# Attention scores and their row maxima from float32r parts of q and k: even and odd heads on the two row halves of the TensorE array, issued in pairs

## What is computed

```python
x = x + _L0_conv_ref(_gn(x), L0_conv_w_qkv, L0_conv_w_o)
x = x + _L1_conv_ref(_gn(x), L1_conv_w1, L1_conv_b1, L1_conv_w2, L1_conv_b2, L1_conv_bias_w, L1_conv_bias_b)

def _L0_conv_ref(x, w_qkv, w_o):
    ...
    attn = jnp.einsum('bhqd,bhkd->bhqk', q, k) * scale      # scale = 16 ** -0.5, n = 1024 tokens
    attn = jax.nn.softmax(attn, axis=-1)
    out = jnp.einsum('bhqk,bhkd->bhqd', attn, v)
    out = out.swapaxes(1, 2).reshape(bs, n, c)
    return out @ w_o
```

## Time and profile before

| | |
|---|---|
| median of three runs | 1689.3 us (1689.0 to 1699.71) |
| profiled execution, first to last instruction (the only time of it that is given) | 1693.3 us |
| TensorE (PE) busy | 1619.6 us, 96% |
| DVE busy | 1242.5 us, 73% |
| ACT busy | 980.5 us, 58% |
| POOL busy | 235.2 us, 14% |
| first score matmul | 71.4 us |
| start of the last score matmul | 1596.2 us |

### The profile page before, as it was taken

How to read it: one execution, slowest core, us unless ns; L and a number is a source line. 1 busy time by engine, 2 the same in 40 slices (tenths; PEclk the granted TensorE clock), 3 DMA queues, 4 the chain that set the end, 5 groups by cost and what they waited for, 6 DMA issues and landing times.

```text
span 1693.3 us, 28191 instructions
## 1 busy us (share of the span) xinstructions
PE 1619.6 (96%) x8580; PEld 692.3 (41%) x8580; DVE 1242.5 (73%) x2236; ACT 980.5 (58%) x1837; POOL 235.2 (14%) x297
## 2 busy tenths in 40 slices
PE   8999999999999999999999999999999999999877
PEld 4233334344343444344343443434444444434345
DVE  2887888777778767877678777877788777787132
ACT  4275776665656655666556665666566666666401
POOL 3001001410104001130013100141011300030010
PEclk9699999999999999999999999999999999999989
DMA  4501113134313134041240430422430412310323
GB/s 109 82 20 38 16 39 82 27 58 83 81 22 58 35 78 101 3 73 48 49 101 2 83 73 14 101 32 54 83 78 7 74 47 48 82 27 22 66 42 77
DMA packets 110733, 93.81 MB, mean 55 GB/s; under 512 B 27632, under 2 KB 96624, under 8 KB 110576
## 3 DMA queue, kind: packets, MB, share of 16 engines
q1 hardware_dynamic: 110576, 91.86, 27.2%
HBM read 14.32 MB, written 6.29 MB: 12 GB/s over the span
## 4 chain that ended last, share of the span: by engine, by line
PE 67%; issue 14%; DVE 6%; POOL 4%; SPq 3%; DMA 3%; ACT 1%; POOLq 0%; DVEq 0%; ACTq 0%
PE o_acc L1168 17%; PE scores L1134 16%; PE max_tiles L1148 15%; DVE row_max L902 3%; PE prep_bank L1239 3%; PE prep_bank L1191 2%; PE post_bank L1303 2%; PE post_bank L1297 2%; SPq L584 2%; PE post_bank L1203 2%; PE post_bank L1310 2%; DMA rows_b<-rows_a 1%; PE post_bank L1289 1%; PE post_bank L1210 1%; PE post_bank L1191 1%
## 5 line engine op out<-in xcount | busy, mean ns | idle before, releaser
L902 DVE TENSOR_REDUCE row_max<-max_tiles 128x1 f32<-128x512 f32 x1536 | 972.6, 680 | 208.7 <-PE max_tiles L1148 205.5
L805 ACT ACTIVATE probs<-scores 128x512 f32<-128x512 f32 x1536 | 837.2, 596 | 368.6 <-PE scores L1134 362.9
L1134 PE MATMUL scores<-q_stack,k_stack 98*128 98x512 bf16 x1536 | 587.3, 384 | 3.1 <-ACT probs L805 2.6
L1148 PE MATMUL max_tiles<-k_stack,q_stack 96*128 96x512 bf16 x1536 | 581.8, 388 | 6.0 <-DVE row_max L902 4.3
L1168 PE MATMUL o_acc<-probs,v_aug 128*32 128x512 f32 x3072 | 413.1, 610 | 13.1 <-ACT o_raw L813 11.9
L1134 PEld LDWEIGHTS scores<-q_stack,k_stack 98*128 98x128 bf16 x1536 | 150.3, 98 | 381.7 <-ACT probs L805 254.7
L1148 PEld LDWEIGHTS max_tiles<-k_stack,q_stack 96*128 96x128 bf16 x1536 | 152.7, 99 | 181.3 <-DVE row_max L902 76.0
L463 POOL TENSOR_TENSOR o_raw<-o_raw,inv_all 128x1024 f32<-128x1024 f32 x23 | 54.2, 2356 | 763.8 <-DVE inv_all L930 763.8
L1168 PEld LDWEIGHTS o_acc<-probs,v_aug 128*32 128x32 f32 x3072 | 60.8, 108 | 160.0 <-issue 144.2
L735 POOL TENSOR_TENSOR qk_parts<-rest,qk_parts 128x512 bf16<-128x512 f32 x48 | 55.5, 1156 | 404.3 <-DVE qk_parts L960 404.3
L1239 PE MATMUL prep_bank<-xt,w_qk 96*128 96x512 f32 x172 | 80.8, 592 | 0.0
(11 more groups left out here) (220 smaller groups left out, 1114.4 us busy)
## 6 DMA issues: line engine op xcount, KB each, us to landing
q_stack<-qk_parts SPq DMA_DIRECT2D x288, 64.0 KB, 2.6
k_stack<-qk_parts SPq DMA_DIRECT2D x144, 128.0 KB, 4.5
rows_b<-rows_a SPq DMA_DIRECT2D x128, 96.0 KB, 3.2
spec_b<-spec_a SPq DMA_DIRECT2D x64, 102.0 KB, 2.3
x_in<-in_x_dram SPq DMA_DIRECT2D x8, 768.0 KB, 5.8
o_t<-o_raw SPq DMA_DIRECT2D x96, 64.0 KB, 2.4
x<-in_x_dram SPq DMA_DIRECT2D x8, 768.0 KB, 6.8
rows_b<-spec_b SPq DMA_DIRECT2D x32, 192.0 KB, 3.3
```

The costliest lines, as they stand in the source:

```text
L805: nc.scalar.activation(probs[:, GH * (s % 2) + h, :], scores[:, n % SCORE_BANKS, :], ACT.Exp, scale=SCALE).then_inc(probs_made, 1)
L902: nc.vector.tensor_reduce(row_max[:, which, pair_of_half:pair_of_half + 1], max_tiles[:, no % MAX_BANKS, :], AX.X, ALU.max).then_inc(max_t ...
L1134: mm(scores[:, n % SCORE_BANKS, :], k_stack[:, head, P * kt:P * (kt + 1)], q_stack[:, g, half, h, :], start=True, stop=True).then_inc(scor ...
L1148: mm(max_tiles[:, no % MAX_BANKS, :], q_stack[0:KQ, g, half, h, P * qt:P * (qt + 1)], k_stack[0:KQ, GH * g + h, HALF * which:HALF * (which ...
```

## The change

- q and k are cut into two float32r parts in place of three bf16 parts. Three products of parts are stacked (`KQ` = 48), with the two shift rows 50.
- A stack holds two heads: even heads on partitions 0 to 49, odd heads on 64 to 113. Each score or maximum matmul then uses 64 rows of the array, the lower or the upper half.
- The order on PE becomes score, score, maximum, maximum, product with v, middle jobs, score, score, maximum, maximum. The two maximum matmuls of a pair are the odd and the even head for the same queries and keys (`max_unit`).
- The evacuation of a q/k job has two operations: ACT writes part 0, DVE writes part 1 straight from the bank. `rest`, the cast and the POOL operation are gone. `stack` waits for DVE in place of POOL.
- `shifts` takes four transfers in place of two. `stack` still takes six, of the same number of bytes.
- The rows of ones come from one DVE memset of `k_stack` in the prologue in place of 12 ACT instructions.

```diff
-Q_PARTS = (0, 0, 0, 1, 1, 2)
-K_PARTS = (0, 1, 2, 0, 1, 0)
+Q_PARTS = (0, 0, 1)
+K_PARTS = (0, 1, 0)
 KQ = HD * len(Q_PARTS)
...
-        qk_parts = sb("qk_parts", [P, 3, 3, TOK], BF16)
-        rest = sb("rest", [P, 2, HALF])
-        q_stack = sb("q_stack", [KQ + 2, NG, 2, GH, HALF], BF16)
-        k_stack = sb("k_stack", [KQ + 2, NH, TOK], BF16)
+        qk_parts = sb("qk_parts", [P, 2, 3, TOK], F32R)
+        q_stack = sb("q_stack", [P, NG, 2, GH // 2, HALF], F32R)
+        k_stack = sb("k_stack", [P, NH // 2, TOK], F32R)
...
+        def max_unit(unit, i):
+
+            half, m = divmod(unit, HUNITS)
+            hp, qt = divmod(m, NT // 2)
+            return half, hp, qt, 1 - i % 2, i // 2
...
-                for n in range(2):
-                    sp.dma_start(q_stack[KQ + n:KQ + n + 1, g, half, :, :],
-                                 shift[:, n, :]).then_inc(shift_in, 16)
+                for n, odd in itertools.product(range(2), range(2)):
+                    row = 64 * odd + KQ + n
+                    sp.dma_start(q_stack[row:row + 1, g, half, :, :].bitcast(F32),
+                                 shift[HMAX // 2 * odd:HMAX // 2 * (odd + 1), n, :].bitcast(F32)
+                                 ).then_inc(shift_in, 16)
...
-            def last_part(b, k):
-
-                pool.wait_ge(part1_done, 6 * b + k + 1)
-                cols = slice(HALF * (k % 2), HALF * (k % 2 + 1))
-                nc.gpsimd.tensor_tensor(qk_parts[:, 2, k // 2, cols], rest[:, k % 2, :],
-                                        qk_parts[:, 1, k // 2, cols], ALU.subtract
-                                        ).then_inc(part2_done, 1)
...
-                head = GH * g + h
-                mm(scores[:, n % SCORE_BANKS, :], k_stack[:, head, P * kt:P * (kt + 1)],
-                   q_stack[:, g, half, h, :],
+                hp, odd = divmod(h, 2)
+                rows = slice(64 * odd, 64 * odd + KQ + 2)
+                mm(scores[:, n % SCORE_BANKS, :], k_stack[rows, 2 * g + hp, P * kt:P * (kt + 1)],
+                   q_stack[rows, g, half, hp, :],
                    start=True, stop=True).then_inc(scores_made, 1)
...
-                    for tile in tiles[0:1]:
+                    score_tile(b, g, s, 0)
+                    score_tile(b, g, s, 1)
+                    for tile in tiles[0:2]:
                         max_tile(*tile)
-                    score_tile(b, g, s, 0)
-                    for tile in tiles[1:2]:
-                        max_tile(*tile)
-                    score_tile(b, g, s, 1)
...
                     score_tile(b, g, s, 2)
-                    for tile in tiles[2:3]:
-                        max_tile(*tile)
                     score_tile(b, g, s, 3)
-                    for tile in tiles[3:]:
+                    for tile in tiles[2:]:
                         max_tile(*tile)
```

More of the change, by code:

```diff
@@ L856, in prologue @@
             def prologue():
-                act.wait_ge(cleared, 3)
-                for head in range(NH):
-                    nc.scalar.activation(k_stack[KQ:KQ + 2, head, :], inv_all[KQ:KQ + 2, :],
-                                         ACT.Identity, bias=1.0).then_inc(stack_ones, 1)
                 for no, (kind, k) in enumerate(PREP):
```

144 lines of the change are left out of this document (65 added, 79 removed).

## The result

The changed kernel takes **1747.2 us**, the median of four runs (1737.6 to 1761.0), against 1690.8 us for the kernel before on the same chip (1689.0 to 1699.7): a ratio of **1.033, 95% interval 1.027 to 1.038**. It is slower, where 1649 us was forecast. The profiled execution has a span of 1759.1 us, 65.8 more than the one of before.

The account below looks back on a forecast made before the run. PE was taken to bound the kernel, with the score loop close behind. Batches together -39 us and prologue -1.6 took the profiled 1693.3 to 1653; less a 4.0 offset, 1649 us, range 1600 to 1735 (likeliest case 1620 to 1672).

Parts of the forecast that it names:

- The score loop: Round of score matmuls and exponentials through two score banks: 2.88 us, rising to about 3.15 in a step without jobs.
- open loads: Weight loads on PE not hidden behind a running matmul: 0.04 us per step, between 0 and 0.15.
- The free room for a first job: PE's wait for exponentials, from third score to the next step's second: 0.95 us of a first job costs nothing.
- its turns: PE's changes between tile shapes: its own step becomes about 2.1 us with them, 1.96 without.
- The sum of a full batch: 48 steps of 3.15 us plus middle jobs, first-job excess and additions: 193.3 us, 10 less than 203.4.
- the 5.8 us added for ACT's copies and for DVE: Added to a full batch: 2.8 us for ACT evacuating middle jobs between exponentials, 3 us for DVE's bunched work.
- the 10 for DVE in batch 0: Added to batch 0 for DVE, making it 173 us, 7.4 more than before.
- the 10 us of batch 3: Gain computed for full batch 3 and given to each of the four batches in the loop.
- The clock: PE's granted clock should stay full, as in batch 7 at 1.00 despite waits; a fall would make the forecast wrong.
- Batch 7: The batch whose last 11 steps have no maximum matmuls: its time stays within 1 us.
- The prologue: Cast and POOL operation ahead of the first stack go: 0.42 + 1.16 = 1.6 us won.
- everything meets everything: Rival: PE, ACT and DVE nearly level, maximum matmuls' bank waits hold up the product with v; 3.3 us, 1718; chance 0.12.

Follow-up runs that it names:

- e5: Changed kernel with the first maximum pair moved between score 0 and score 1, ahead of the second score matmul: 1731.1 us, ratio 1.021 to the kernel before.
- e1: Kernel before, bf16 on all rows, with only PE's order changed to score, score, maximum, maximum: 1750.8 us, ratio 1.035.
- e9: Changed kernel with every score and maximum matmul on all 128 rows, none side by side: 1788.4 us, ratio 1.058 to the kernel before.
- e12: Kernel before, bf16 and its own order, with score and maximum matmuls on only 34 and 32 rows: 2948.3 us, ratio 1.74.
- e3: Changed kernel with all score and maximum matmuls on the lower half of the array, none side by side: 2372.5 us, ratio 1.40 to the kernel before.

## Why the prediction was wrong

**The score loop: right mechanism, mis-sized.** The prediction took 2.88 us + 0.22 for the maximum pair + 0.04 for open loads = 3.15. Measured: 3.33. The pair costs 0.24 (e5 against the changed kernel, and 3.33 against the 3.10 of a step without maximum matmuls). The other term is the one that failed: "I take 0.04 us per step for it, between 0 and 0.15". It is 0.22, for two loads stand open in every round of the loop, not now and then: that of the second score, which waits for its exponential, and that of the third score behind the product with v (0.43 and 0.53 in place of 0.32 and 0.43). A load of 0.11 us waits with its matmul, as the PEld rows show; 0.11 is the price that the earlier trace rows had given. In e1, with bf16, no such term appears (3.32 = 2.88 + 0.44); with float32r on all rows it does (3.10 in place of 2.88 in batch 7 of e9). It belongs to float32r, not to the halves.

**The free room for a first job: mis-sized.** It was put at 0.95 us, so a step with a q/k product should take 3.15 + 1.72 - 0.95 = 3.92. It takes 4.41. PE's own work in such a step, without the job, is 2.50 + 0.19 = 2.69 us where the prediction had "about 2.1" with its turns: the score behind a job starts 1.91 behind it in place of 1.72, the first pair behind a job has its load open (0.34), the pair behind the product with v waits for the exponential or its load (0.42), and from the last maximum pair to the job it is 0.43, against 0.21 from maximum matmul to job before. From a maximum pair to the product with v it is 0.32, which is nothing new: it was 0.31 from a score of all rows. In the terms of the prediction the room is 3.33 - 2.69 = 0.64. The Trainium skill (TensorEngine Tiling (Array Packing), Key Properties) says that a change of the tiling mode drains the engine. The trace agrees where shapes alternate: matmuls of 34 and 32 rows start 0.32 apart in e12, those of one shape 0.22, and halves in place of all rows cost 0.4 us in a step with a q/k product (e3 against e9). The prediction gave all its turns together 0.14.

**The sum of a full batch.** Batch 2 ran at the full clock throughout: 199.3 us, against 203.4 before and 193.3 forecast. With the two sizes put right it would be 48 x 3.33 + 19.5 + (16.7 + 20 x 0.31) = 202.2; the 5.8 us added for ACT's copies and for DVE aren't there, nor most of the 10 for DVE in batch 0 (168.8 in e5, at a clock of 0.96). That the sum comes within 3 us is therefore partly luck, as errors cancel in it. Over 384 steps the loop's 0.18 is at most 69 us, against a forecast gain of 39. The forecast also gave each batch of the loop the 10 us of batch 3. But batches 4 and 5 took 199.4 and 196.2 us before, not 203.4, so the same 193.3 would have been a gain of 6 and 3. And its base of 2.84 us for a step without jobs holds for a single one; in a row they take 2.93.

**The clock: the step that failed as reasoning.** "The granted clock should stay full: in batch 7 it is 1.00 although PE waits in each step". The row was right and the conclusion wrong: it showed that waits of PE do not lower the clock while its matmuls use 98 rows, and e1 confirms that. The change altered the rows as well, and no row of before had a stretch with few rows to tell what that does; the term was put at nothing. It costs 33 to 47 us by the estimate above. That few rows lower the clock is shown by e3 and e9; that this is what happens in the changed kernel is argued from them. The prediction did name a fall of the clock as what would make it wrong, but gave it no price and no chance.

**Batch 7** was to stay within 1 us and lost 19.7. About twenty of its steps have no first job and lose up to 0.5 each, which the prediction had computed for full batches and not applied here; of the rest about 10 are the clock (0.92).

**Right:** the pairs, in the main: the third and fourth score start within 0.01 us of one another in the median, and so do the maximum matmuls, though 219 of the 768 maximum pairs are over 0.1 apart; float32r at the rate of bf16 within 7%; the first two scores of a waiting step 0.48 apart; PE's longest waits those for ACT, though ACT's waits for PE did not go but grew; loads of the same half hidden. No wait for the shift's extra transfers is among the longest. **The prologue** won more than the 1.6 us forecast: 6.2. The last part of the last q/k piece was written by 31.35 us (30.66 + 0.69 on DVE) and not by 37.94 (36.78 + 1.16 on POOL). The removed operations had spaced the pieces: POOL's last two started 1.71 us apart, at 35.07 and 36.78, and there are six such pieces in a row. The prediction counted the two operations once.

**The rivals.** The forecast's own rival "everything meets everything" gave 3.3 us per step and 1718, near to the 1712 that the clock of before would have left by the estimate above. Its number was nearly right by luck, through another cause: open loads, not waits for DVE.

## What to carry to other kernels

In a loop that goes through two engines and few banks, price an instruction by where it stands, not by how busy its engine is: a matmul pair between the waited-for score and the product with v cost 0.24 us a step, the same pair one place earlier nothing. A wait on a matmul opens its weight load: in a loop bound by waits add the full load for each waited-for matmul (0.11 us here for float32r), even where a dense series hides it. Matmuls of unlike row counts that alternate pay for each turn, 0.10 us in e12. And before splitting matmuls of 96 rows into pairs of 48, set the gain against the clock: here side by side saved some 75 us and the granted clock took back about half, both by estimate.

## What the runs showed of the hardware that was not expected

- PE's granted clock went with the rows of its matmuls: 0.985 with 128 rows and 0.746 with 48 to 50 for the same columns and order; 0.977 with 96 to 98 and 0.608 with 32 to 34 in turn in the kernel before, although PE was busy 99% of the span. What counts (rows, products, the half of the array, or something that goes with them) is open; so is why the long stretch at the lower level comes in batch 0 in the profiled execution of the changed kernel and in batch 7 in that of e5.
- Each us at the lower level cost about 0.32 us in the changed kernel, not 0.5, as much of each step is a wait for ACT. In batch 0 of e3, all of it at the lower level, it was 0.42 (320.4 us against 186.5 in e9).
- float32r at 512 columns took 0.230 us against 0.216 for bf16, on one half, on 128 rows, and per pair on both halves; its load of 128 columns 0.11 us where it was open.
- Matmuls of 34 and 32 rows in turn started 0.32 us apart, matmuls of one shape 0.22 (bf16, 512 columns): each change of shape left the load open.
